# Filtering in two wide fp32 matmuls per frequency and building NF4 code masks in packed pairs on ScalarE and VectorE, in a two-layer tower

## The reference

```python
A = exp(A_abslog + 1j * A_phase); dtA = log(A)
Cc = (x[..., 0] + 1j * x[..., 1]) * (A - 1.0) / dtA
h = 2 * einsum('chn,hnl->chl', Cc, exp(dtA[:, :, None] * arange(1024))).real
h = h + attention(layernorm(h))                       # 16 heads of 64, rotary, causal
h = h + layernorm(h) @ (NF4_CODE[w_idx] * absmax).T + bias    # a code and its block's absmax per weight
h = h + mamba(layernorm(h))                           # 2048 channels, 16 states, conv of 4 taps, scan over 64
h = h + moe_lora(layernorm(h))                        # base matmul, router top 2 of 8, rank 16
```

## Time and profile before

| | us |
|---|---|
| median of 3 runs | 4660.4 (4654.24 to 4661.36) |
| the profiled execution's own time | 4654.98 |
| its span, first to last instruction | 4653.2 |
| TensorE busy, whole span | 4288.1 (92%) |
| VectorE / ScalarE / GpSimd busy | 2944.0 / 1925.1 / 2374.1 |
| first matmul of L850, the first on a weight strip | at 472.97 |

### The profile page before, as it was taken

How to read it: one execution, slowest core, us unless ns; L and a number is a source line. 1 busy time by engine, 2 the same in 40 slices (tenths; PEclk the granted TensorE clock), 3 DMA queues, 4 the chain that set the end, 5 groups by cost and what they waited for, 6 DMA issues and landing times.

```text
span 4653.2 us, 61881 instructions
## 1 busy us (share of the span) xinstructions
PE 4288.1 (92%) x23384; PEld 2834.9 (61%) x23408; DVE 2944.0 (63%) x3095; ACT 1925.1 (41%) x2873; POOL 2374.1 (51%) x1017
## 2 busy tenths in 40 slices
PE   0886999999999999999999999999999999999999
PEld 0654777754457777754357777754457777754457
DVE  7896546459953446459953446459953536469953
ACT  1111223467732223467732223367732223367731
POOL 3443333358863333358863333358863333368862
PEclk9898999999998999999998999999998999999998
DMA  1113222310022222320022222310022222310021
GB/s 41 37 37 124 71 72 71 121 65 16 14 73 85 86 69 68 121 65 16 14 73 86 84 71 68 121 65 16 14 76 83 86 69 72 121 63 14 16 75 64
DMA packets 95229, 302.70 MB, mean 65 GB/s; under 512 B 11408, under 2 KB 15632, under 8 KB 92688
## 3 DMA queue, kind: packets, MB, share of 16 engines
q1 hardware_dynamic: 85776, 282.62, 18.6%
q10 hardware_dynamic: 9216, 16.78, 1.0%
HBM read 253.22 MB, written 46.14 MB: 64 GB/s over the span
## 4 chain that ended last, share of the span: by engine, by line
PE 81%; DVE 13%; issue 2%; ACT 1%; POOL 1%; DMA 1%; SPq 0%; DVEq 0%; ACTq 0%; POOLq 0%
PE psg L823 38%; PE psx L998 9%; PE psg L1013 7%; DVE sb_wst L1492 6%; PE psg L850 5%; PE psx L838 3%; PE psg L859 2%; PE psx L805 2%; PE psx L929 1%; PE psg L1027 1%; PE psg L812 1%; PE psx L942 1%; PE psg L975 1%; PE psx L1040 1%; PE psg L1024 1%
## 5 line engine op out<-in xcount | busy, mean ns | idle before, releaser
L505 POOL TENSOR_TENSOR sb_wl<-sb_raw,sb_wh 128x1024 fp32r<-128x1024 f32 x388 | 973.0, 2511 | 1841.1 <-ACT sb_wh L572 1841.0
L1492 DVE TENSOR_TENSOR_SCAN sb_wst<-sb_dA,psx 128x1024 f32<-128x1024 f32 x512 | 1140.2, 2271 | 37.7 <-ACT sb_dA L695 23.7
L998 PEld LDWEIGHTS psx<-sb_dgB,sb_duT 64*128 64x128 f32 x4096 | 359.2, 189 | 526.2 <-DVE sb_wst L1492 263.6
L695 ACT ACTIVATE sb_dA<-sb_dlt,sb_a_sb 128x504 f32<-128x504 f32 x1024 | 646.4, 704 | 60.6 <-DVE sb_wst L1492 54.8
L998 PE MATMUL psx<-sb_dgB,sb_duT 64*128 64x256 f32 x4096 | 591.9, 409 | 85.7 <-DVE sb_wst L1492 83.9
L572 ACT ACTIVATE sb_wh<-sb_raw 128x1024 fp32r<-128x1024 f32 x388 | 408.2, 1053 | 616.5 <-PE psg L823 330.8
L539 POOL TENSOR_TENSOR sb_wst<-sb_wst,sb_cb_lo 128x1024 f32<-128x1024 f32 x256 | 599.4, 2364 | 90.2 <-DVE sb_wst L1492 90.1
L539 POOL TENSOR_TENSOR sb_wst<-sb_wst,sb_cb_hi 128x1024 f32<-128x1024 f32 x256 | 598.2, 2357 | 76.2 <-DVE sb_wst L1492 76.2
L1013 PE MATMUL psg<-sb_wst,sb_cst 64*64 64x512 f32 x4096 | 564.3, 624 | 10.3 <-POOL sb_wst L539 9.6
L823 PE MATMUL psg<-sb_xh,sb_wh 128*128 128x512 f32 x2112 | 557.9, 407 | 0.0
L823 PE MATMUL psg<-sb_xh,sb_wl 128*128 128x512 f32 x2112 | 522.2, 389 | 0.0
(11 more groups left out here) (250 smaller groups left out, 5823.1 us busy)
## 6 DMA issues: line engine op xcount, KB each, us to landing
sb_raw<-in_w SPq DMA_DIRECT2D x360, 512.0 KB, 3.3
sb_raw<-w_ffn_dequantized SPq DMA_DIRECT2D x32, 512.0 KB, 3.3
gates<-sb_gt ACTq DMA_DIRECT2D x64, 256.0 KB, 2.5
sb_gin<-gates SPq DMA_DIRECT2D x64, 256.0 KB, 2.7
h_after_tok<-sb_hT SPq DMA_DIRECT2D x4, 2048.0 KB, 14.6
sb_u<-h_after_tok SPq DMA_DIRECT2D x4, 2048.0 KB, 8.1
h_after_tok<-sb_h SPq DMA_DIRECT2D x4, 2048.0 KB, 8.4
sb_h<-h_after_tok SPq DMA_DIRECT2D x4, 2048.0 KB, 7.9
```

Source lines behind the costliest of these rows:

```text
L505: pool.tensor_tensor(rest(b, i0), raw[:, i0 % RAW, :, :], high(b, i0).bitcast(F32), ALU.subtract).then_inc(s_wl, 1)
L695: ins_ = A(dA[:, (m * NQ + k) % RING, :, n, 1:S], dlt[:, m % 2, :].rearrange("p (b s) -> p b s", b=NB)[:, :, 1:S], ACT.Exp, scale=a_sb[:, ...
L998: ins_ = mm(psx[:, 2 * j + r, :].rearrange("p (a t e) -> p a t e", a=8, e=2)[:, :, :, e], duT[r0:r0 + 64, m % 2, i * P:(i + 1) * P], dgB[r ...
L1492: v.tensor_tensor_scan(wst[:, x, 4 * j:4 * j + 4, :, :].rearrange("p b n s -> p (b n s)"), dA[:, x, 4 * j:4 * j + 4, :, :].rearrange("p b ...
```

## The change

- **Filter.** t is split as t = 128 a + 32 b + c: 32 low powers (`tab`, now two tables), and short tables `tabs` of 4 middle and 8 high powers (two tables of 12). For a group of FG = 8 frequencies VectorE makes `low`, the 128 values of t mod 128 (three instructions of 1024 elements), and `high_`, coefficients times the 8 high powers for all sequences (eight instructions of 512), for real and imaginary part. TensorE does, per frequency, two fp32 matmuls with 256 columns that accumulate, so that 8 chunks x 32 sequences come out at once. ScalarE copies two frequencies at a time to `hT`. There are two sets of coefficients. GpSimd does nothing in this stage any more.
- **Masks.** Two codes share an instruction: `dqi` holds the same 64 rows twice, in the lower and the upper 64 partitions, and the 128 rows of a half as two runs of 512. One instruction (128 x 1024) compares the lower partitions with one code, the upper with the other, taken per partition. Of the 8 pairs VectorE makes 5 (ring of 3), ScalarE 3 (ring of 2), each by Abs(x - code) and Relu(1 - that). A part is a 128 x 64 matrix with a diagonal for each code, and two matmuls, one for each run of 512, write 64 output partitions each. There are 22 parts. The matrices come from DRAM.
- **Order.** Loops over halves are written out. Five halves (EARLY) run between the steps of the set-up, the other eleven between the 8 filter groups (LATE). On VectorE: table 0, masks(0), table 1, masks(1), the short tables, `gco` and the inputs of the exponentials, masks(2), then a wait for ScalarE's exponentials and the products, masks(3), `gco` and gmix, masks(4), both coefficient sets, powers(0). masks(i) ends with weights(i - 1), the product by absmax, which waits for `s_useda`. On ScalarE: masks(0), sine of table 0, masks(1), sine of table 1, masks(2), sines of the short tables and `gco`, all exponentials, masks(3), masks(4). TensorE takes in each half VectorE's five pairs first, then ScalarE's three. On SP the four `mode` loads and const come first; on GpSimd `dg`, `kmul` and the wait for `s_h0` are gone.
- **Layout.** `hT` is ordered by block, and its block 0 lies where `u` will be, which layer 1 reads through `block_in`. SP loads two strips first, then stores blocks 2, 3 and 1, then loads the next two strips. VectorE's centring waits for the stores of 2 and 3 (`s_keep`).

The diff, cut to its core:

```diff
-            hT = sb("hT", [P, KC, NSEQ, S], F32, c)
+            hT = sb("hT", [P, NBLK, KC, NB, S], F32, c)
+            mka = sb("mka", [P, RING_ACT, 2, HALF], BF16, c)
+            mkd = sb("mkd", [P, RING_DVE, 2, HALF], BF16, c)
+            away = sb("away", [P, 2, 2, HALF], BF16, c)
+PAIRS, BY_ACT, BY_DVE, RING_ACT, RING_DVE, FG, EARLY = 8, 3, 5, 2, 3, 8, 5
+LATE = [[5, 6], [7], [8, 9], [10], [11, 12], [13], [14], [15]]
+        def block_in(b, k):
+            return u[:, k, :] if b else hT[:, 0, k, :, :].rearrange("p b s -> p (b s)")
@@ SP @@
+            load_codes(0)
+            sp.dma_start(dg[:, :, :].rearrange("p n c -> p (n c)"), ins["dg"]).then_inc(s_diag, 16)
+            load_codes(1)
+            for q in range(2):
+                load_absmax(q)
...
+            for i in range(HALVES):
+                if i + 2 < HALVES:
+                    sp.wait_ge(s_dqf, i + 1)
+                    load_codes(i + 2)
+                sp.wait_ge(s_dq, i + 1)
+                sp.dma_start(w_ffn[m, :, q * HALF:(q + 1) * HALF], dqw[:, q, :]).then_inc(s_dqw[q], 16)
+                if i + 2 < HALVES:
+                    load_absmax(i + 2)
+            sp.wait_ge(s_hT, S // 2)
-                    sp.dma_start(u[:, 0:KC, :], h0[0]).then_inc(s_h, 16)
-                        first_strips(0)
+                        first_strips(0, 0, 2)
+                        for n in (2, 3, 1):
+                            sp.dma_start(h0[n], hT[:, n, :, :, :].rearrange("p k b s -> p k (b s)")).then_inc(s_keep if n > 1 else s_h0, 16)
+                        first_strips(0, 2, 4)
+                        sp.wait_ge(s_h0, 16)
+                        sp.wait_ge(s_keep, 32)
@@ ScalarE @@
+            def masks(i):
+                act.wait_ge(s_dqi[q], i // 2 * 32 + 32)
+                if i >= 2:
+                    act.wait_ge(s_mkd, (i - 1) * BY_DVE)
+                A(dqf[:, q, :, :], dqi[:, q, :, :], ACT.Copy).then_inc(s_dqf, 1)
+                act.wait_ge(s_dqf, i + 1)
+                for j in range(BY_ACT):
+                    at = i * BY_ACT + j
...
+                    A(away[:, at % 2, :, :], dqf[:, q, :, :], ACT.Abs, bias=C("minus", BY_DVE + j, 1)).then_inc(s_away, 1)
+                    act.wait_ge(s_away, at + 1)
+                    if at >= RING_ACT:
+                        act.wait_ge(s_useda, at - RING_ACT + 1)
+                    A(mka[:, at % RING_ACT, :, :], away[:, at % 2, :, :], ACT.Relu, bias=C("one"), scale=-1.0).then_inc(s_mka, 1)
+            def copies(g):
+                for n in range(4 * g, 4 * g + 4):
+                    act.wait_ge(s_filt, n + 1)
+                    A(hT[:, :, :, :, 2 * n:2 * n + 2].rearrange("p b k c e -> p (b k c) e"),
+                      psg[:, n % 4, :].rearrange("p (e x) -> p x e", e=2), ACT.Copy).then_inc(s_hT, 1)
...
+            for g in range(S // FG):
+                for i in LATE[g]:
+                    masks(i)
+                copies(g)
@@ TensorE @@
+            def dequant(i):
+                if i >= 2:
+                    pe.wait_ge(s_dq, i - 1)
+                def codes(n, mask, first, last):
+                    for part in range(PART0[n], PART0[n + 1]):
+                        for r in range(2):
+                            ins_ = mm(psx[64 * r:64 * r + 64, q, :], dg[:, part, :].bitcast(BF16), mask[:, r, :],
+                                      start=(first and part == PART0[n]), stop=(last and part == PART0[n + 1] - 1))
+                    return ins_
+                for j in range(BY_DVE):
+                    at = i * BY_DVE + j
+                    pe.wait_ge(s_mkd, at + 1)
+                    codes(j, mkd[:, at % RING_DVE, :, :], j == 0, False).then_inc(s_usedd, 1)
...
+            def filters(g):
+                pe.wait_ge(s_px, g + 1)
+                for n in range(FG // 2):
+                    at = g * FG // 2 + n
+                    if at >= 4:
+                        pe.wait_ge(s_hT, at - 3)
+                    for e in range(2):
+                        for part in range(2):
+                            ins_ = mm(psg[:, at % 4, 256 * e:256 * e + 256], low[:, g % 2, 2 * n + e, :, :].rearrange("p a b -> p (a b)"),
+                                      high_[:, g % 2, part, 2 * n + e, :, :, :].rearrange("p b k c -> p (b k c)"),
+                                      start=(part == 0), stop=(part == 1))
+                    ins_.then_inc(s_filt, 1)
+            for i in range(EARLY):
+                dequant(i)
+            for g in range(S // FG):
+                filters(g)
+                for i in LATE[g]:
+                    dequant(i)
@@ VectorE @@
+            def masks(i):
+                v.wait_ge(s_dqf, i + 1)
+                for j in range(BY_DVE):
+                    at = i * BY_DVE + j
+                    if at >= RING_DVE:
+                        v.wait_ge(s_usedd, at - RING_DVE + 1)
+                    ts(mkd[:, at % RING_DVE, :, :], dqf[:, q, :, :], C("code", j, 1), None, ALU.is_equal).then_inc(s_mkd, 1)
+                if i >= 1:
+                    weights(i - 1)
...
+            def powers(g):
+                if g >= 2:
+                    v.wait_ge(s_filt, (g - 1) * FG // 2)
+                for e in range(2):
+                    for blk in range(NBLK):
+                        tt(high_[:, g % 2, e, :, blk, :, :],
+                           coef[:, e, a:z, blk * NB:(blk + 1) * NB].unsqueeze(2).to_broadcast([P, FG, KC, NB]),
+                           tabs[:, e, a:z, 4:12].unsqueeze(3).to_broadcast([P, FG, KC, NB]), ALU.mult)
+                if g >= 1:
+                    v.wait_ge(s_px, g)
+                own.link(tt(low_im[:, :, :, :], *low_of(1), ALU.mult))
+                own.link(tt(low[:, g % 2, :, :, :], *low_of(0), ALU.mult))
+                tt(low[:, g % 2, :, :, :], low[:, g % 2, :, :, :], low_im[:, :, :, :], ALU.add).then_inc(s_px, 1)
+            powers(0)
+            for g in range(S // FG):
+                if g + 1 < S // FG:
+                    powers(g + 1)
+                for i in LATE[g]:
+                    masks(i)
+            weights(HALVES - 1)
...
+                    if L == 0:
+                        v.wait_ge(s_keep, 32)
+                        v.wait_ge(s_cst, 16 * 6)
```

More of the change, by code:

```diff
@@ L85, in constants @@
     re, im = np.r_[np.ones(64), np.zeros(64)], np.r_[np.zeros(64), np.ones(64)]
-    put("phase", np.stack([0.25 * re, 0.25 * im, np.full(P, 0.25), 0.5 * re], 1))
-    put("phase_rad", np.stack([0.25 * re, 0.25 * im, np.full(P, 0.25), 0.5 * re], 1) * 2 * np.pi)
+    put("phase", np.stack([0.25 * re, 0.25 * im, np.full(P, 0.25), 0.5 * re, 0.5 * im], 1))
+    put("phase_rad", np.stack([0.25 * re, 0.25 * im, np.full(P, 0.25), 0.5 * re, 0.5 * im], 1) * 2 * np.pi)
     put("half_pi", np.full((P, 1), np.pi / 2))
-    put("gmix", np.stack([2 * re, -2 * im, -2 * im, -2 * re], 1))
+    put("gmix", np.stack([2 * re, -2 * im, -2 * im, -2 * re, 2 * im, -2 * re, -2 * re, -2 * im], 1))
     put("t32", np.tile(np.arange(32), (P, 1)))
-    put("t32x32", np.tile(32 * np.arange(32), (P, 1)))
+    put("t12", np.tile(np.r_[32 * np.arange(4), 128 * np.arange(8)], (P, 1)))
+    pair = np.array([[(CODES + [(-1, 0.0)])[2 * p + c][0] for p in range(8)] for c in range(2)])
+    put("code", np.repeat(pair, 64, 0))
+    put("minus", -np.repeat(pair, 64, 0))
     row = np.arange(P)[:, None]
@@ L128, with pair_parts, code_diagonals @@
 CODES = [(i, c) for i, c in enumerate(NF4) if c != 0.0]
-MASKS = 6
-HALF = KC * P // 2
+CONST_ARRAY = constants()
+NCONST = CONST_ARRAY.shape[1]
+PAIRS = 8
+BY_ACT = 3
+BY_DVE = PAIRS - BY_ACT
+RING_ACT, RING_DVE = 2, 3
+HALF = KC * P // 2
+HALVES = 2 * KC
+FG = 8
+EARLY = 5
+LATE = [[5, 6], [7], [8, 9], [10], [11, 12], [13], [14], [15]]
+def pair_parts(p):
+    two = [bf16_parts(c) for _, c in (CODES + [(-1, 0.0)])[2 * p:2 * p + 2]]
+    return [(a, b) for a, b in zip(*two) if a or b]
+PART0 = [sum(len(pair_parts(p)) for p in range(n)) for n in range(PAIRS + 1)]
+def code_diagonals():
+    parts = [part for p in range(PAIRS) for part in pair_parts(p)]
+    bits = (np.array(parts, np.float32).view(np.uint32) >> 16).astype(np.uint16)
+    return (np.eye(64, dtype=np.uint16)[None, :, None, :] * bits.T[:, None, :, None]).reshape(P, -1)
 def strip_use(i0, jj, n):
@@ L549, in _ @@
             act.sem_inc(s_strip, CR_STRIP)
[L550 to L565 removed]
+            act.wait_ge(s_mode, 80)
@@ new lines, in copies @@
+            def copies(g):
[3 more added lines that the diff above has]
+                      psg[:, n % 4, :].rearrange("p (e x) -> p x e", e=2), ACT.Copy).then_inc(s_hT, 1)
+            masks(0)
+            act.wait_ge(s_tab, TAB_SIN[0])
+            A(tab[:, 0, :, :], tab[:, 0, :, :], ACT.Sin, bias=0.0).then_inc(s_tabA, 1)
+            masks(1)
@@ new lines, in _ @@
+            act.wait_ge(s_tab, TAB_SIN[1])
+            A(tab[:, 1, :, :], tab[:, 1, :, :], ACT.Sin, bias=0.0).then_inc(s_tabA, 1)
+            masks(2)
+            act.wait_ge(s_tab, TAB_SIN[2])
```

(20 more changed lines are left out.)

269 lines of the change are left out of this document (108 added, 161 removed).

## The result

The changed kernel takes 4457.8 us (median of 4 runs, 4456.5 to 4474.4), the kernel before 4658.6 on the same chip: a ratio of 0.9578, with a 95% interval of 0.9554 to 0.9602 (the quotient of the two medians is 0.9569). One of the four runs took 4474.4 us, at a mean granted clock of 0.921 where the others had 0.963. The forecast was 4481, so the sign and the kind of gain were right and the gain was 23 us larger than forecast.

A forecast was written before the change was run, and what follows sets the result against it. The stage before L850's first matmul (472.97 us) was taken as the bound: first filter 117, loop 149 plus 2 to 268, tail 25.5 to 293.5, 179.5 earlier; 4475.5 plus 5.4 for the median gives 4481 us, range 4442 to 4528.

The forecast's parts named there:

- Set-up: VectorE's work before the loop: start 7.5, own work 72, five halves 20, wait 8, powers(0) 9; first filter matmul at 117 us.
- VectorE's mask: One mask of 1024 bf16 elements with a per-partition code on VectorE was put at 0.45 us.
- Rival (c): VectorE's masks run at 1.2 us: +19 ahead of the loop, +8 in it, 4508 us; chance 0.07.
- Rival (d): ScalarE is the bound: Abs and Relu 1.9 us each, a half 12.5, loop 171 instead of 149, 4503; chance 0.06.
- the step that was mis-sized: TensorE's mask matmuls: 64-column pairs run side by side at 0.276 us, 0.83 a code pair, 6.1 a half.
- The sentence on the Trainium skill: On TensorE's masks: up to 2x for 64 columns against no Fast Weight Load; fast rate 16 x 1.0 us shorter.
- The end of a group: In the loop, the third Relu waits for ScalarE's ring (1.15 us), TensorE uses it (0.83), then the next filters start.
- The clock: TensorE's clock in the loop stays about 0.91, so its 12.7 us become 14.1 and a group 15.4.
- The tail: From hT complete at 268 to L850's matmul: 25.5 us, three stores 16.5 of them; low end 18.5.
- (b): TensorE's 64-column bf16 matmuls run serially at 0.23 us each: about +45 in the loop, +5 ahead, 4531; chance 0.09.
- (e): Slower than before: 64-column matmuls neither overlap nor run at full clock, 0.43 us each, 4681; chance 0.02.
- The range's low end, 4442: Whole run: pair at 0.23 (-7), full clock (-11), tail 18.5 (-7), wait of 4 (-4), 10 off set-up and group 0 waits.

## Why the prediction was right, and where 23 us went

**Set-up: held.** Measured: start 6.94 for the 7.5 predicted, 21.3 us for the five halves for the 20 (3.9 for the first, 4.2 to 4.5 for the others, with their waits), a wait of 9.12 for the 8, the first filter at 117.36 for 117. The wait came where it was put, at L1335, behind ScalarE's third mask; removing that mask's wait removed it.

**VectorE's mask: held.** Predicted 0.45, measured 0.40 from start to start (484 ns each). Rival (c) at 1.2 is out. **ScalarE: held.** Abs and Relu 1.14 and 1.15, a half 7.8 for the 8.1 assumed, a copy 0.60 for 0.7. Rival (d) is out: it took the rate of the strided copy for Abs and Relu, which at 1.9 us each would have been far from the 1.14 and 1.15 measured, and in the loop ScalarE waits for TensorE.

**TensorE: the step that was mis-sized.** Pairs side by side were right, and so was a third Relu that waits near the end of the group. But "I take 0.276 a pair: 0.83 a code pair" came from L1013, and the mask matmuls ran at 0.109 each, 0.218 a pair: 0.65 for a code pair of three parts, which is what 0.83 stood for. That is below even the low end of 0.23. L1013 was the wrong neighbour, and the trace of before shows why. Its passes are 64 rows by 64 columns and f32. Four of them start within 40 ns, the next four 0.48 us later or more, and after eight there is a pause (near 999 us, for example). Busy time divided by count, 0.138 us, holds the end of the last passes of each short burst; it is not the rate of an unbroken row.

The sentence on the Trainium skill had set a fast and a slow rate against each other. The first (the Trainium skill, "TensorEngine Tiling (Array Packing)", theoretical speedup: up to 2x for 64 columns; it does not stand under performance considerations, where the prediction put it) is borne out by this trace: 3.26 us against 6.29 for thirty is a factor of 1.93. The second (the Trainium skill, the same page, restrictions and gotchas: no Fast Weight Load with column tiling) fits the traces too. A bf16 load of 64 columns takes 106 to 110 ns, and one of 128 columns took 95 to 98 before (L805). But it costs nothing here, since the loads lie under the matmuls.

**The end of a group: a wait that was left out.** The prediction had the last code pair, 0.83 us, between the third Relu and the next filters. In the trace the last code pair has one part only, and what stands there is ScalarE's copy, 0.59 us. That this did not cost the forecast more is luck: the copy that was left out takes about as long as the code pair that was put in its place.

**The clock: a wrong carry-over.** "If the clock stays about 0.91, as from 200 to 300 us" did not hold: it was 0.99 from 120 to 200 us and 1.00 after. The prediction's group was 13.9 us at full clock and 15.4 at 0.91. Its own numbers give less, 12.7 / 0.91 + 1.15 = 15.1, so 1.2 of the 1.5 us are the clock and 0.3 a slip of the sum. The measured group is 13.04. Of the 2.35 us by which it was too long, 1.2 are then the clock, 0.3 the slip, 0.8 the six code pairs (4.98 for the 4.18 from 147.67 to 151.85) and 0.2 the last step, while filters and Relu were 0.2 too short. Seven groups make 16.4 us of it; group 0 (23.2 for 25) gives 1.8, the two second halves (7.75 for 8.2) 0.9, the last copies 0.5, and the set-up takes 0.4 back: with the rounding of that sum, 19.1 between 268 and 248.87.

**The tail: held.** 25.5 predicted, 25.3 measured. That the third strip ends it was right too; moving its load ahead of the third store brought the first strip matmul 5.0 us forward. The 16.5 us for three stores had no stated source: three quarters of 23.7 are 17.8, and three quarters of the 21.1 measured with the layout part undone are 15.8. The range's 18.5, with the strip overtaking the third store, is out: on one queue it did not.

**The rest.** 19.3 of the 23 us are the loop and the tail. The other four are no part of the stage: the sum added the 5.4 us by which the runs' median stood above the one profiled execution, and here the profiled execution stands at the median (4457.9 against 4457.8). Of that, 1.7 went back: what follows L923 is 1.0 longer, and what lies outside the span is 2.5 instead of 1.8.

**Rivals.** (b), built by hand, cost 45 us where it said 50, and is not what the pairs do. (e), slower than before, would have needed 0.40 us a matmul; they took 0.109. The range's low end, 4442, counted a full clock, cheap pairs, a shorter tail and shorter waits in the set-up together; the first two came, the others only by edits of buffers and queue, and so the result lies between it and the forecast. The errors in the rate, the clock and the median had one sign, which is how they came to 23 us.

## What to carry to other kernels

Where one engine makes a buffer that another uses, write down who waits for the buffer in the turn in which all buffers are full: here a ring of two on a side engine held TensorE once a group and, through its in-order queue, held back exponentials that VectorE needed, 25 us for 2 KB a partition. Follow each engine's queue past that buffer, too: here it was the copy behind the late Relu that let the next group begin. Take a rate from a row in which the instruction isn't waiting (start to start, in an unbroken stretch), since busy time divided by count holds the end of each burst, and look at the shape of the work around it before its clock is carried over to a loop that does something else. And among transfers on one queue, put what the next engine waits for ahead of what nobody waits for.
